# Splitting fp32 matmuls into column halves of the array (128x512 into four of 64x256)

## What is computed

```python
def _cin_forward(x, ws, bs):                      # x: (512, 39, 16)
    prev = x
    for k in range(3):
        z = einsum('bmd,bhd->bdmh', x, prev)      # 39 x 39, then 39 x 128 products
        t = einsum('bdc,co->bdo', z, ws[k]) + bs[k]   # 128 units
        t = transpose(t, (0, 2, 1))
        t = t / sqrt(sum(t * t, axis=(-2, -1)))
        logit.append(t); prev = t
    return sum(concatenate(logit, axis=1), axis=-1)   # (512, 384)
z = _cin_forward(e, [w0, w1, w2], [b0, b1, b2])
h = relu(concatenate([z, dense_ctx]) @ W_top1 + b_top1)
h = relu(h @ W_top2 + b_top2)
y = h @ W_top3
```

## Time and profile before

| what | value |
|---|---|
| median of 3 runs | 1243.46 us |
| the profiled execution, its own time | 1242.94 us |
| its span, first to last instruction | 1240.9 us |
| TensorE (PE) busy | 1201.1 us, 97% |
| weight loads (PEld) busy | 531.4 us, 43% |
| VectorE (DVE) busy | 877.9 us, 71% |
| granted TensorE clock, mean | 0.997 |
| one tile of the loop | 73.18 us |

### The profile page before, as it was taken

The page is one execution under the profiler, slowest core; times in us unless marked ns, Lnnn a source line. Parts: engine busy times, 40 slices in busy tenths (PEclk is TensorE's granted clock), DMA queues, the critical chain, the costliest instruction groups (busy, mean ns, idle before and its releaser), DMA issues.

```text
span 1240.9 us, 9676 instructions
## 1 busy us (share of the span) xinstructions
PE 1201.1 (97%) x2808; PEld 531.4 (43%) x2808; DVE 877.9 (71%) x748; ACT 81.6 (7%) x139; POOL 157.5 (13%) x183
## 2 busy tenths in 40 slices
PE   0899999999999999999999999999999999999999
PEld 0334444444444444444444444444444444444443
DVE  1657787677687777768678677867767876876671
ACT  0010010101001010000101000010100001010002
POOL 5130203020030301103030120303002030000000
PEclk9899999999999999999999999999999999999999
DMA  4988275461826647183563718356271745627000
GB/s 96 400 247 298 58 248 148 176 216 58 280 62 223 172 152 226 50 287 76 196 200 126 233 39 281 111 177 218 100 245 50 260 135 177 215 69 260 0 1 0
DMA packets 92574, 203.70 MB, mean 164 GB/s; under 512 B 41756, under 2 KB 49692, under 8 KB 92567
## 3 DMA queue, kind: packets, MB, share of 16 engines
q1 hardware_dynamic: 85786, 202.08, 49.6%
q0 software_dynamic: 5120, 1.29, 1.3%
q10 hardware_dynamic: 1660, 0.25, 0.1%
HBM read 201.67 MB, written 1.90 MB: 164 GB/s over the span
## 4 chain that ended last, share of the span: by engine, by line
PE 93%; SPq 4%; DMA 1%; POOL 1%; issue 1%; DVE 0%; ACT 0%; POOLq 0%
PE acc L464 84%; PE acc L448 7%; SPq L218 1%; SPq L188 1%; SPq L210 1%; POOL gathered L167 1%; PE t_ps L515 1%; SPq L203 1%; DMA xr<-xt 1%; DMA xt<-gathered 0%; PE acc L505 0%; PE nrm_ps L474 0%; DMA gathered<-in_table,rows_of 0%; SPq L190 0%; DMA base_sb<-in_base 0%
## 5 line engine op out<-in xcount | busy, mean ns | idle before, releaser
L464 PE MATMUL acc<-z,w_sb 128*128 128x512 f32 x2496 | 1079.6, 593 | 6.8 <-DVE z L353 6.7
L353 DVE TENSOR_TENSOR z<-t_ps,xb 128x1536 f32<-128x1536 f32 x416 | 709.0, 1752 | 227.8 <-PE acc L464 142.1
L464 PEld LDWEIGHTS acc<-z,w_sb 128*128 128x128 f32 x2496 | 473.5, 190 | 597.9 <-issue 571.4
L167 POOL DMA_INDIRECT gathered<-in_table,rows_of x160 | 152.8, 955 | 60.8 <-issue 47.8
L448 PE MATMUL acc<-xr,w_sb 117*128 117x512 f32 (+1 forms) x224 | 102.6, 609 | 29.3 <-issue 28.6
L161 POOL TENSOR_TENSOR rows_of<-ids_sb,base_sb 128x10 int32<-128x10 int32 x16 | 3.3, 205 | 795.4 <-DMA xt<-gathered 793.9
L339 DVE TENSOR_TENSOR xr<-x,xr 117x512 f32<-117x512 f32 (+1 forms) x112 | 69.0, 686 | 31.4 <-DMA x<-xt 18.3
L448 PEld LDWEIGHTS acc<-xr,w_sb 117*128 117x128 f32 (+1 forms) x224 | 43.3, 195 | 85.4 <-issue 82.9
L378 DVE RECIPROCAL inv<-root 128x96 f32<-128x96 f32 (+2 forms) x18 | 12.4, 687 | 60.9 <-ACT root L292 60.8
L280 ACT ACTIVATE t_ps<-acc,bias 128x512 f32<-128x512 f32 x16 | 10.6, 662 | 461.1 <-PE acc L464 421.2
L268 ACT ACTIVATE sq<-scaled,bias 128x512 f32<-128x512 f32 x16 | 11.6, 722 | 387.8 <-issue 268.8
(11 more groups left out here) (41 smaller groups left out, 53.6 us busy)
## 6 DMA issues: line engine op xcount, KB each, us to landing
xb<-xt SPq DMA_DIRECT2D x208, 768.0 KB, 6.3
xr<-xt SPq DMA_DIRECT2D x144, 156.0 KB
x<-xt SPq DMA_DIRECT2D x45, 78.0 KB
gathered<-in_table,rows_of POOLq DMA_INDIRECT x160
xr<-xt SPq DMA_DIRECT2D x32, 78.0 KB
w_sb<-in_w SPq DMA_DIRECT2D x13, 192.0 KB, 10.3
xt<-gathered SPq DMA_DIRECT2D x16, 72.0 KB, 6.9
wt_sb<-in_wt SPq DMA_DIRECT2D x1, 768.0 KB
```

Source lines behind the costliest of these rows:

```text
L167: nc.gpsimd.indirect_dma_start(gathered[0:n, g, :], None, table[:, :], bass.IndirectOffsetOnAxis(rows_of[0:n, g:g + 1], 0)).then_inc(rows_ ...
L353: nc.vector.tensor_tensor(z[:, s % ZSLOTS, :, :], fields_of(k), xb[:, c * CH:(c + 1) * CH, :], ALU.mult).then_inc(z_ready, 1)
L464: last = nc.tensor.matmul(acc[k][:, :], w_sb[k][:, m, :], z[:, s % ZSLOTS, r, :], start=(m == 0), stop=(m == FIELDS - 1))
```

## The change

Layers 1 and 2: every 128 x 512 matmul becomes four. Each takes 64 of the 128 weight columns (so it writes 64 of the 128 partitions of `acc[k]`) and 256 of the 512 moving columns. The order is: first 256 columns with the lower 64 units, the same with the upper 64 units, and then the same two for the last 256 columns. Layer 0 and the norms' matmul are issued as two halves of 64 units over all their moving columns. The dense tower is as it was. Waits, semaphores and the work of the other engines are unchanged.

```diff
+HALVES = (slice(0, UNITS // 2), slice(UNITS // 2, UNITS))
...
-                    last = nc.tensor.matmul(acc[0][:, :], w0_sb[0:n, k, :], xr[0:n, k, :],
-                                            start=(k == 0), stop=(k == STEPS0 - 1))
+                    for o in HALVES:
+                        last = nc.tensor.matmul(acc[0][o, :], w0_sb[0:n, k, o], xr[0:n, k, :],
+                                                start=(k == 0), stop=(k == STEPS0 - 1))
...
                     for r in range(CH):
                         m = CH * c + r
-                        last = nc.tensor.matmul(acc[k][:, :], w_sb[k][:, m, :], z[:, s % ZSLOTS, r, :],
-                                                start=(m == 0), stop=(m == FIELDS - 1))
+                        for h in range(2):
+                            cols = slice(h * N // 2, (h + 1) * N // 2)
+                            for o in HALVES:
+
+                                last = nc.tensor.matmul(acc[k][o, cols], w_sb[k][:, m, o],
+                                                        z[:, s % ZSLOTS, r, cols],
+                                                        start=(m == 0 and h == 0),
+                                                        stop=(m == FIELDS - 1 and h == 1),
+                                                        skip_group_check=True)
                     last.then_inc(z_used, 1)
...
-                nc.tensor.matmul(nrm_ps[:, k0 * TILE_B:k1 * TILE_B], ones[:, :],
-                                 ssum[:, k0:k1, :].rearrange("p k b -> p (k b)"),
-                                 start=True, stop=True).then_inc(nrm_ready, 1)
+                for o in HALVES:
+                    last = nc.tensor.matmul(nrm_ps[o, k0 * TILE_B:k1 * TILE_B], ones[:, o],
+                                            ssum[:, k0:k1, :].rearrange("p k b -> p (k b)"),
+                                            start=True, stop=True)
+                last.then_inc(nrm_ready, 1)
```

## The result

The changed kernel takes 1250.36 us (median of 3 runs, 1249.87 to 1252.0) against 1243.46 before. The ratio is 1.0046, 95% interval 1.0032 to 1.0059: slower by 4 to 7 us. The forecast was slower, but 3000 us, in a range from 1400 to 3250. The time came out at the second rival (the array bounds, the halves overlap: 1249), which had been given 7 in 100.

A forecast was written before the change was run, and what follows sets the result against it. The array bounds the kernel before; after the change the sequencer would, at 0.52 us a matmul. Start 43, tile 0 180, fourteen loop tiles 2590, tile 15 168, tower 25, and 2 make 3008, said as 3000 us; range 1400 to 3250.

The forecast's parts named there:

- the second rival: Layers 1 and 2: array bounds, halves overlap, if the sequencer takes under 0.216 us a matmul; +6 us, 1249; chance 0.07.
- What bounds it now: Kernel before: TensorE's array is the bound, busy 97% of the span; a layer 1 or 2 matmul costs two passes, 0.858 us.
- That price: ... 0.52 us each: Sequencer handing matmuls to the array: (1.66 - 0.1)/3 = 0.52 us per matmul, whatever its width; 170.6 us a loop tile.
- The first chunks of tile 0: Start of tile 0: three chunks 1.67 us apart, taken as the sequencer's same pace, since the array's slow clock couldn't set it.
- Its stalls: Sequencer standing still twice a tile, after the branch and at 391.5 to 398.3: 10 us a tile, no longer hidden.
- A fetch, which I held for likelier: At the sequencer's two standstills a tile: it waits for further instructions to be fetched; together up to 24 us a tile.
- The array: Passes over 256 columns in layers 1 and 2: 0.216 us each, so 0.216 to 0.432 us per new matmul.
- A rule weighed: Skill's 62 ns per MATMUL, giving 0.12 to 0.25 us a matmul and near 1249, set aside for the trace row's 0.52.
- One half after the other: Layers 1 and 2: array bounds, halves don't overlap, 1.727 us for 0.858; 2424 us in all; chance 0.08.
- Loads not pulled ahead: Layers 1 and 2: halves overlap but weight loads hold them up, 0.27 us a matmul; about 1530 us; chance 0.10.
- Faster: Between passes: the other half's pass fills the 0.0025 us gap, 7 us saved, so 1237; chance 0.11.

The follow-up runs named there:

- the run with short products: Against the kernel before: VectorE builds only one field of three of each chunk from tile 1 on (the others are stale); 1242.54 us, ratio 0.9987.

## Why the prediction was wrong

*"What bounds it now"*, the array, was right, and so was its arithmetic: a pass is its columns at two cycles and 2.5 ns more. The runs give 0.429, 0.216 and 0.110 us at 512, 256 and 128 columns (54.10/126, 54.39/252, 2.63/24).

*"That price: ... 0.52 us each"* is the step that failed. I took the interval between two register instructions as time in which the sequencer worked. It waited: the instruction after each L461 waits for `z_ready`, which VectorE raises. VectorE's row in the very stretch of the earlier trace rows, 325.1 to 333.4, which I didn't ask for, is

```profile
L353 DVE TENSOR_TENSOR z<-t_ps,xb 128x1536 f32<-128x1536 f32 x5 | 8.4, 1751 | 0.0
```

five products for five chunks, back to back, at the pace that I gave to the sequencer. The first chunks of tile 0 were no check on it: what I had excluded there was the array's clock, and not VectorE. With 12 matmuls a chunk the changed kernel's first interval there is much the same, 1.7 us:

```profile
L464 PEldq EVENT_SEMAPHORE  x3: 51/51/51, 43.1 to 48.3; - x3
```

(They start at 43.1, 44.8 and 48.3. VectorE's products there end every 1.73 us, the third at 46.5, so the last interval isn't its.) The run with short products shows it directly. What the runs showed in the price's place is at most 0.058 us a matmul: the sequencer stays under the array's 0.216, and the array bounds.

*"Its stalls"* have the same cause. At 391.5 to 398.3 VectorE normalizes and begins the next product at 396.44, and the sequencer goes on at that product's end; after the branch the product begins at 338.46 and ends at 340.2, and the sequencer goes on at 340.3:

```profile
395.84 0.69 DVE L396 TENSOR_TENSOR t_ps<-traw,rnorm 128x512 f32<-128x512 f32 x1
396.44 3.42 DVE L353 TENSOR_TENSOR z<-t_ps,xb 128x1536 f32<-128x1536 f32 x2
```

```profile
338.46 1.76 DVE L353 TENSOR_TENSOR z<-t_ps,xb 128x1536 f32<-128x1536 f32 x1 [5.14 <-PE acc L464]
```

A fetch, which I held for likelier, isn't needed there. By the branch and the instruction queue's traffic it seems to count in the kernels whose loop body is twice and four times the changed kernel's. (The 87 matmuls of a tile before are 86: 78, 7 and 1. It changes nothing.)

*"The array"*: the bounds of 0.216 and 0.432 a matmul were right, and the lower one holds, since the halves lie in different column groups (the run without that took 2298). The rival's sum, +6 us and 1249, was within 2 us of the median. Written with the rounded 0.216 and 0.858 it gives 7.5; unrounded (0.2158 and 0.8583) it is 6.

*"A rule weighed"*: I let the misread row overrule the Trainium skill (TensorE: Matmul & The Clock Gate, section "Wait — 56ns, not 53.3ns?"), and should have kept both open: a matmul here is two MATMULs, and 0.058 us for both is even under its 62 ns each, which fits its case of decoding in hardware. The same page's Part 3 has a line by which loads overlap matmuls only for other row groups. It isn't borne out: both halves use all rows, and at 0.108 us a pass no load holds up a pass of the other half. The same part also lets a load for the background weight buffer go ahead, which would fit; no run here tells.

*The rivals.* One half after the other: needed a common column group. Loads not pulled ahead: no sign, with passes over 64 columns at 0.058 us each. Faster: refuted, the 2.5 ns belong to each half's own passes, as halves of 512 columns were neither faster nor slower (1.0003).

## What to carry to other kernels

A sequencer's interval is a price only where its next instruction waits for nothing. Before it is multiplied, look at what the engine that raises the semaphore did in the same stretch; equal paces mean a wait. Splitting an fp32 matmul into two column halves cost nothing measurable here and brought nothing, as long as no more than about four passes of one half stood in a row in the program and nothing between them used the whole array. Splitting its moving columns costs 2.5 ns for every pass added in a row, so wide passes are the better form.

## What the runs showed of the hardware

- Passes of the two column halves don't begin in program order: four of one half and then four of the other overlapped fully, and with 12 or 24 in a row 3.5 to 3.8 at each change did.
- A turn between whole array and halves costs 0.18 us in the mean (74.24 against 73.52 us a tile, four turns).
- The loop's branch takes 0.21 us with a body of 86 or 328 matmuls. In the median it takes 3.6 with 640 and 4.8 with 1264 (6.2 at most), while the instruction queue's traffic goes from 0.26 MB at 328 to 3.05 and 5.55.
- After a stop of PE of 2.45 us the granted clock was 0.53 for the next 3.4 us (an estimated 1.5 us more lost), and 0.50 for 3 us after one of 5.86 us.
